# A decoder block on one core: the masked key planes of cross-attention made by GpSimd from one ScalarE copy

## The chip, the cores and the metric

One core of a Trainium2 chip runs the whole kernel. The metric is the device time of one execution in microseconds (us); lower is better. Three executions of the kernel before took 1203.84, 1200.0 and 1203.6 us, median 1203.6.

## The reference, cut to what matters

128 sequences of 64 tokens, width 128, all fp32. Three sublayers, each on a layer norm of x and added back to x:

```python
x = x + agent_attention(layernorm(x))          # 16 heads of 64, 8 pooled agents
x = x + cross_attention(layernorm(x), ctx)     # 16 heads of 8, causal
x = x + moe(layernorm(x))                      # gate, top 2 of 16 experts, 2 shared experts

# cross attention
Q, K, V = split(query @ Wq.T), split(key @ Wk.T), split(value @ Wv.T)   # (B, 16, 64, 8)
scores = Q @ K^T / sqrt(8) + causal
out = softmax(scores) @ V, heads joined, @ Wo.T
```

The change is in how K reaches the scores.

## The kernel before

**Groups.** The work is cut into 8 groups of 16 sequences (1024 tokens). The function `both(e, g)` of each engine runs one step of a two-stage pipeline: group g passes through both attentions while group e = g - 1 passes through the experts. So there are 9 steps: one with g = 0 alone, seven with both, one with e = 7 alone. Each engine (PE, DVE, ACT, POOL, and SP for loads) has its own fixed order written out by hand, and the engines meet through semaphores. An engine that waits holds everything behind it on its own queue.

**PSUM rings.** Results of PE lie in eight banks, shared out in rings. The ring "att" has four banks; `KT_0` and `KT_1` (the transposed keys, 128 x 512 each, all 16 heads by 8 rows) are two of its tenants. PE may fill a bank again when the semaphore in the table `read` says that the tenant before has been read: for `KT_n` that is `Kx_ready`.

**Keys.** The score matmuls (L602 to L605) contract over 32 rows at a time, in which four heads of 8 rows lie. So that a head meets only its own 8 rows, K is stored four times, in planes `Kx[:, j, :]` of the tile `KQ` (planes 0 to 3), each with the rows of the other heads set to zero and those of its own scaled by 8^-0.5. ScalarE makes them in `K_moved(g, n)` (L869 to L877): for each half n (512 tokens), four `activation(Copy)` from PSUM with a scale of one value per partition, `plane[:, j]`. The queries go to `Qx`, plane 4 of `KQ`, in `Q_moved` (L900), late in the step.

**Order on ACT** around the keys: ctxT, V and xnT1 moves; `K_moved(g, 0)`; `M_moved` 0 to 3 (moments of agent attention); the two xnT3 moves with their fp32r roundings (L940, L941); `M_moved` 4; the exponential of the gate (L946); `M_moved` 5 to 7; `silu(e, 0)`; `K_moved(g, 1)`; `silu(e, 1)`; the move of combS.

**Order on PE**: `keys_of(g, 0)` (L660), `moments` 0 to 3 (L668), xnT3, moment 4, gate logits (L708), moments 5 to 7, `unit(e, 0)` (L488 to L490), agent scores (L538, L549), `keys_of(g, 1)`, `up(e, 1)`, `down_to(e, 0)` (L507), then the transposes of combS (L726), which wait for `comb_ready`, and with combsT back from ACT the expert units 1, 2, 3 and on.

**Order on DVE**: add_x, the norms (L1036 to L1046), pooled (L1229), xn3, `gate_shift` (L1058), `gate` (L1066 to L1117), then `soften(g, 0)` (L1144) and the hidden units. `gate(e)` picks the top two experts in a serial chain of some thirty small instructions; after L1083 it runs `hidden(e, 0)` (L1128), which waits for `silu(e, 0)`. Its last instruction, L1117, raises `comb_ready`. Most of its instructions are `tensor_tensor` with both inputs in SBUF:

```python
link_e(V.tensor_tensor(orig[:], gex[:], g2[:].unsqueeze(2).to_broadcast(te), ALU.mult))   # L1075
link_e(V.tensor_tensor(sc[:], orig[:], gb[:].unsqueeze(1).to_broadcast(te), ALU.add))     # L1076
```

Their `link` is a semaphore wait of DVE on its own instruction.

**Order on POOL**: the power for the norm of g (L393), the power for the norm of e (L396), the low parts of xnT3 (L400, two halves), `xr = xin + bo` (L409), store 0 of e (L388), a power (L415), store 1, then the 32 normalisations of the cross-attention probabilities (L423).

Of the kernel before, what the change touches and what calls it, by code (L numbers as in the profile page):

```python
# [6 lines left out]
def decoder_block(nc, x, ctx_in, Wqkv, Wo_a, bo, Wq, Wk, Wv, Wo_x, gate_w, gate_b,  # L7
# [14 lines left out]
    ALU, ACT, AX = mybir.AluOpType, mybir.ActivationFunctionType, mybir.AxisListType.X  # L22

    B, S, D = x.shape
    P = 128
# [14 lines left out]
    CH = 512  # L40
# [39 lines left out]
    with ExitStack() as ctx:  # L80
# [3 lines left out]
        def sem(name):  # L84
            return ctx.enter_context(nc.semaphore(name))
# [127 lines left out]
        var3_ready, rstd3_ready, xn3_ready, xnT3_ready = (  # L213
            sem("var3_ready"), sem("rstd3_ready"), sem("xn3_ready"), sem("xnT3_ready"))
        w_split, hi_ready, lo_ready = sem("w_split"), sem("hi_ready"), sem("lo_ready")
        ctxT_ready, Kx_ready, V_ready = sem("ctxT_ready"), sem("Kx_ready"), sem("V_ready")
        pooled_ready, M_ready = sem("pooled_ready"), sem("M_ready")
        d1_ready, d2_ready, e1_ready, e2_ready = sem("d1_ready"), sem("d2_ready"), sem("e1_ready"), sem("e2_ready")
        p2_ready, p1T_ready, p2T_ready = sem("p2_ready"), sem("p1T_ready"), sem("p2T_ready")
# [14 lines left out]
                "combT_1": (combT_ready, 3, 2)}  # L234
        for n in range(2):
            read |= {f"xnT1_{n}": (xnT_ready, 4, n), f"xnT2_{n}": (xnT_ready, 4, 2 + n),
                     f"xnT3_{n}": (hi_ready, 2, n), f"ctxT_{n}": (ctxT_ready, 2, n), f"KT_{n}": (Kx_ready, 2, n),
                     f"QT_{n}": (Qx_ready, 2, n), f"Y_{n}": (out_ready, 2, n), f"s2_{n}": (d2_ready, 2, n),
                     f"p1T_{n}": (p1T_ready, 2, n), f"p2T_{n}": (p2T_ready, 2, n), f"Ya_{n}": (attn_added, 2, n)}
        for n in range(4):  # L240
# [19 lines left out]
        def ps(name):  # L260

            return bank[place[name][0]][place[name][1]]
# [15 lines left out]
        def wait_full(eng, g, name):  # L278

            ring, k, use, per, _ = place[name]  # L280
            eng.wait_ge(full[ring, k], g * per + use + 1)
# [54 lines left out]
        @block.gpsimd  # L336
        def _(pool):
            steps = [0]

            def step(ins):  # L340
                steps[0] += 1
                ins.then_inc(const_step, 1)
                pool.wait_ge(const_step, steps[0])

            step(nc.gpsimd.memset(b2x[:], 0.0))
            nc.gpsimd.memset(mhalf[:], -0.5).then_inc(consts, 1)
            nc.gpsimd.memset(ident[:], 0.0)
            nc.gpsimd.memset(onehot3[:], 0.0)
            nc.gpsimd.memset(pick[:], 0.0)
            nc.gpsimd.memset(maskb[:], 0.0)  # L350
            nc.gpsimd.memset(beats[:], 0.0)
            step(nc.gpsimd.memset(planes[:], X_SCALE))

            step(nc.gpsimd.affine_select(out=ident[:], in_=ident[:], compare_op=ALU.not_equal, fill=1.0, base=0,
                                         pattern=[[-1, P]], channel_multiplier=1))
            nc.gpsimd.tensor_copy(identb[:], ident[:]).then_inc(consts, 1)
            nc.gpsimd.memset(woM[:], 0.0)
            nc.gpsimd.memset(Vb[:], 0.0)
            nc.gpsimd.memset(xnT[:, TOK:TOK + S], 0.0)
            nc.gpsimd.memset(combs[:], 0.0)  # L360
            nc.gpsimd.memset(combT[:], 0.0)
            step(nc.gpsimd.memset(comb[:], 0.0))
            nc.gpsimd.memset(comb[:, :, E:E + 1], 1.0)
            nc.gpsimd.iota(down[:], pattern=[[-1, E]], base=E, channel_multiplier=0,
                           allow_small_or_imprecise_dtypes=True)

            for k in range(3):
                step(nc.gpsimd.affine_select(out=onehot3[:], in_=onehot3[:], compare_op=ALU.not_equal, fill=1.0,
                                             base=-E * k, pattern=[[-1, E]], channel_multiplier=1))

            step(nc.gpsimd.affine_select(out=planes[:], in_=planes[:], compare_op=ALU.is_ge, fill=0.0, base=0,
                                         pattern=[[-XC, 4], [-4 * XC, 4]], channel_multiplier=1))
            step(nc.gpsimd.affine_select(out=planes[:], in_=planes[:], compare_op=ALU.is_ge, fill=0.0, base=XC - 1,
                                         pattern=[[XC, 4], [4 * XC, 4]], channel_multiplier=-1))
            for q in range(XQ):
                rr = slice(32 * q, 32 * q + 32)
                for a in range(2):
                    step(nc.gpsimd.affine_select(out=maskb[rr, a], in_=maskb[rr, a], compare_op=ALU.is_ge, fill=MASKED,
                                                 base=32 * a, pattern=[[0, HALF], [-1, S]], channel_multiplier=1))
                    step(nc.gpsimd.affine_select(out=pick[rr, a], in_=pick[rr, a], compare_op=ALU.not_equal, fill=1.0,  # L380
                                                 base=32 * a, pattern=[[-1, S]], channel_multiplier=1))
            nc.gpsimd.tensor_copy(spread[:].rearrange("r p a i -> r (p a) i"),
                                  onehot3[:].unsqueeze(2).to_broadcast([P, E, EI])).then_inc(consts, 1)

            def store(e, c):
                pool.wait_ge(out_ready, CHUNKS * e + c + 1)
                dst = o_v[e] if isinstance(e, int) else o_v[bass.ds(e, 1)].rearrange("a p t d -> (a p) t d")
                pool.dma_start(dst[:, QT * c:QT * c + QT, :], xo[:, QT * c:QT * c + QT, :]).then_inc(stored, 16)  # L388

            def both(e, g):  # L390
                if g is not None:
                    pool.wait_ge(var_ready, 2 * g + 1)
                    nc.gpsimd.tensor_tensor(rstda[:], va[:], mhalf[:], ALU.pow).then_inc(rstd_ready, 1)  # L393
                if e is not None:
                    pool.wait_ge(var3_ready, e + 1)
                    nc.gpsimd.tensor_tensor(rstdb[:], vb[:], mhalf[:], ALU.pow).then_inc(rstd3_ready, 1)  # L396
                    for n in range(2):
                        half = slice(512 * n, 512 * n + 512)
                        pool.wait_ge(hi_ready, 2 * e + n + 1)
                        nc.gpsimd.tensor_tensor(xnT3l[:, half], xnT3[:, half], xnT3h[:, half].bitcast(fp32),  # L400
                                                ALU.subtract).then_inc(lo_ready, 1)
                if g is not None:

                    pool.wait_ge(xn_ready, 2 * g + 1)
                    if e is not None:
                        pool.wait_ge(xattn_added, UX * g)
                    else:
                        pool.wait_ge(loaded_m, 16 * 10)
                    nc.gpsimd.tensor_tensor(xr[:], xin[:], bo_b[:].unsqueeze(1).to_broadcast([P, T, D]),  # L409
                                            ALU.add).then_inc(xr_ready, 1)  # L410
                if e is not None:
                    store(e, 0)
                if g is not None:
                    pool.wait_ge(var_ready, 2 * g + 2)
                    nc.gpsimd.tensor_tensor(rstda[:], va[:], mhalf[:], ALU.pow).then_inc(rstd_ready, 1)  # L415
                if e is not None:
                    store(e, 1)
                if g is not None:
                    for k in range(XQ * UX):
                        u, q = k // XQ, k % XQ  # L420
                        pool.wait_ge(rx_ready, 2 * UX * g + k // 2 + 1)
                        p = pr[k % PR]
                        nc.gpsimd.tensor_tensor(p, p, rx[:, u % 2, q].unsqueeze(2).to_broadcast([P, HALF, S]),  # L423
                                                ALU.mult).then_inc(pn_ready, 1)

            run(pool, both)
            pool.wait_ge(stored, 16 * CHUNKS * GROUPS)


        @block.tensor  # L430
        def _(pe):
# [240 lines left out]
            def both(e, g):  # L672
# [116 lines left out]
                    pe.wait_ge(loaded_m, 16 * 10)  # L789
                    pe.wait_ge(w_split, 4)  # L790
                if g is not None:
                    pe.wait_ge(Kx_ready, 2 * g + 2)
                    pe.wait_ge(V_ready, 4 * g + 4)
                    scores(g, 0)
                if e is not None:
# [22 lines left out]
        def _(act):  # L818
# [50 lines left out]
            def K_moved(g, n):  # L869

                if isinstance(g, int) and g == 0:
                    act.wait_ge(w_split, 4)
                wait_full(act, g, f"KT_{n}")
                for j in range(4):
                    last = nc.scalar.activation(Kx[:, j, 512 * n:512 * n + 512], ps(f"KT_{n}")[:], ACT.Copy,
                                                scale=plane[:, j:j + 1])
                last.then_inc(Kx_ready, 1)  # L877

            def V_moved(g, n):

# [18 lines left out]

            def Q_moved(g, n):  # L900

                moved(g, f"QT_{n}", Qx[:, 512 * n:512 * n + 512], Qx_ready)

            def exp_x(g, k):
# [411 lines left out]
```

## Time and profile before

| | |
|---|---|
| median of 3 executions | 1203.6 us (1200.0 to 1203.84) |
| the profiled execution, its own time | 1206.25 us |
| its span in the profile | 1204.3 us |
| busy: PE | 980.4 us, 81% |
| busy: DVE | 778.2 us, 65% |
| busy: ACT | 578.7 us, 48% |
| busy: POOL | 237.2 us, 20% |
| mean granted TensorE clock | 0.918 of full speed |

The span is the time between the first and the last instruction; the profiled execution's own time is 1.95 us longer. Seven steps with both stages take about 140 us each. A row of a timeline gives the start, the time from the start of the first to the end of the last instruction of the row, the engine, the line of the kernel, the operation, output and input tile, the count, and in brackets how long the engine stood idle before and what released it.

### The profile page before, as it was taken

What the parts mean: (1) busy time and instruction counts of PE and PEld (TensorE: products, weight loads), DVE (VectorE), ACT (ScalarE), POOL (GpSimd) and SP (SyncE); (2) the same over time, 40 slices, a digit from 0 to 9 for tenths busy, and PEclk for the clock granted to TensorE, in tenths of its full rate; (3) what the DMA queues carried; (4) which work ended last, traced back from release to release, by engine and by line L of the source; (5) the groups of instructions that cost most, each with busy time, mean ns of one, the idle gap of its engine ahead of it and who ended that gap; (6) DMA issues with size and microseconds to landing.
All of it is one profiled execution on the core that took longest, in us unless ns stands there. A gap on an engine that the chain in (4) does not pass through costs nothing.

```text
span 1204.3 us, 24165 instructions
## 1 busy us (share of the span) xinstructions
PE 980.4 (81%) x9023; PEld 777.9 (65%) x9069; DVE 778.2 (65%) x1825; ACT 578.7 (48%) x1148; POOL 237.2 (20%) x236
## 2 busy tenths in 40 slices
PE   6656889968898688977899688977899778996677
PEld 5543678747785477845787376855778457874466
DVE  3356766675657767676666857677676766668454
ACT  4434645365444564355553664445643564536222
POOL 6001410043000520014100440005200241004200
PEclk9887889988899898989899898998989898998789
DMA  5300010000100010000100001000100000000000
GB/s 141 76 1 1 2 36 1 10 10 3 36 9 10 2 37 1 10 10 3 36 1 10 10 3 36 10 10 3 37 1 10 10 4 1 1 10 9 1 1 18
DMA packets 28925, 18.64 MB, mean 15 GB/s; under 512 B 7649, under 2 KB 27394, under 8 KB 28802
## 3 DMA queue, kind: packets, MB, share of 16 engines
q1 hardware_dynamic: 26914, 12.48, 3.9%
q0 software_dynamic: 1280, 4.20, 1.1%
q8 instruction: 84, 1.38, 0.5%
q14 instruction: 39, 0.32, 0.1%
q10 hardware_dynamic: 608, 0.27, 0.1%
HBM read 12.62 MB, written 4.19 MB: 14 GB/s over the span
## 4 chain that ended last, share of the span: by engine, by line
PE 48%; DVE 17%; issue 17%; POOL 9%; ACT 6%; SPq 1%; DMA 0%; DVEq 0%; POOLq 0%; ACTq 0%
PE banks L507 8%; PE banks L488 6%; PE banks L668 5%; POOL PXUT L423 5%; PE banks L490 4%; PE banks L489 4%; PE banks L750 2%; POOL KQ L423 2%; DVE stats_a L1036 2%; DVE mx L1183 2%; PE banks L578 2%; DVE lx L1195 2%; PE banks L497 1%; PE banks L708 1%; PE banks L538 1%
## 5 line engine op out<-in xcount | busy, mean ns | idle before, releaser
L855 ACT ACTIVATE sil<-banks,b 128x512 f32<-128x512 f32 x144 | 99.6, 692 | 209.6 <-PE banks L490 207.5
L1131 DVE SCALAR_TENSOR_TENSOR sil<-banks,b,sil 128x512 f32<-128x512 f32 x128 | 95.9, 749 | 102.1 <-ACT sil L855 90.0
L507 PEld LDWEIGHTS banks<-w,hT 128*128 128x128 f32 x1152 | 156.6, 198 | 7.8 <-issue 2.7
L507 PE MATMUL banks<-w,hT 128*128 128x128 f32 x1152 | 156.9, 280 | 3.1 <-DVE hT L1135 0.5
L848 ACT COPY M<-banks 128x512 f32<-128x512 f32 x208 | 125.0, 613 | 32.3 <-PE banks L668 15.5
L388 POOL DMA_DIRECT2D out_x<-xn x16 | 12.9, 809 | 565.6 <-DVE xn L1141 565.6
L423 POOL TENSOR_TENSOR PXUT<-PXUT,rx 128x512 f32<-128x512 f32 x96 | 97.0, 1040 | 126.9 <-DVE rx L1197 126.9
L1135 DVE TENSOR_TENSOR hT<-sil,banks 128x512 f32<-128x512 f32 x128 | 87.9, 687 | 19.1 <-DVE sil L1131 3.3
L618 PE MATMUL banks<-ident,PXUT 128*128 128x128 f32 x384 | 66.2, 311 | 36.7 <-ACT M L848 32.0
L488 PE MATMUL banks<-xnT3l,w1h 128*128 128x512 f32 x144 | 78.0, 542 | 12.7 <-ACT combsT L848 10.3
L618 PEld LDWEIGHTS banks<-ident,PXUT 128*128 128x128 f32 x384 | 46.1, 155 | 58.5 <-POOL PXUT L423 35.4
L595 PE MATMUL banks<-maskb,pick 32*64 32x512 bf16 x512 | 42.2, 504 | 48.7 <-ACT PXUT L911 27.6
L668 PE MATMUL banks<-pooled,A 128*128 128x128 f32 x512 | 66.5, 290 | 16.1 <-DVE pooled L1229 16.1
L668 PEld LDWEIGHTS banks<-pooled,A 128*128 128x128 f32 x512 | 63.2, 204 | 22.7 <-DVE pooled L1229 22.7
L1183 DVE TENSOR_REDUCE mx<-banks 128x8 f32<-128x512 f32 x96 | 65.2, 679 | 0.0
L488 PE MATMUL banks<-xnT3l,w3h 128*128 128x512 f32 x144 | 61.1, 425 | 4.6 <-DVE sil L1131 4.6
L911 ACT ACTIVATE PXUT<-banks,mx 128x64 f32<-128x64 f32 x192 | 42.0, 330 | 46.0 <-DVE mx L1181 46.0
L848 ACT COPY PXUT<-banks 128x512 f32<-128x512 f32 x64 | 36.0, 588 | 54.8 <-PE banks L578 32.5
L1195 DVE TENSOR_REDUCE lx<-PXUT 128x8 f32<-128x512 f32 x96 | 59.6, 662 | 0.0
L1201 DVE TENSOR_TENSOR xe<-xr,banks 128x256 f32<-128x256 f32 x32 | 13.4, 420 | 71.2 <-PE banks L642 53.8
L490 PE MATMUL banks<-xnT3h,w1h 128*128 128x512 f32 x144 | 59.1, 410 | 0.0
L490 PE MATMUL banks<-xnT3h,w3h 128*128 128x512 f32 x144 | 59.0, 410 | 0.0
(197 smaller groups left out, 2102.4 us busy)
## 6 DMA issues: line engine op xcount, KB each, us to landing
xin<-in_x SPq DMA_DIRECT2D x8, 512.0 KB, 3.9
cin<-in_ctx SPq DMA_DIRECT2D x8, 512.0 KB, 5.0
out_x<-xn POOLq DMA_DIRECT2D x16, 256.0 KB, 2.8
KQ<-in_L_attn_Wqkv SPq DMA_DIRECT2D x3, 512.0 KB, 5.1
KQ<-in_L_ffn_We SPq DMA_DIRECT2D x2, 512.0 KB, 4.6
KQ<-in_L_attn_Wo SPq DMA_DIRECT2D x1, 512.0 KB, 7.7
w<-in_L_ffn_We SPq DMA_DIRECT2D x1, 512.0 KB
woM<-xwT SPq DMA_DIRECT2D x16, 8.0 KB, 1.8
```

What stands on the lines that cost most here:

```text
L423: nc.gpsimd.tensor_tensor(p, p, rx[:, u % 2, q].unsqueeze(2).to_broadcast([P, HALF, S]), ALU.mult).then_inc(pn_ready, 1)
L488: mm(ps(name)[:], wh[:, 2 * p:2 * p + 2, :], xl, start=True, stop=False)
L490: mm(ps(name)[:], wh[:, 2 * p:2 * p + 2, :], xh, start=False, stop=True).then_inc(fulled(name), 1)
L507: mm(ps(name)[:, P * t:P * t + P], hT[:, k % 2, P * t:P * t + P], w2[:, pair[k], :], start=(n == 0 and t == 0), stop=False, skip_group_che ...
L618: last = turn_over(ps(name)[:, P * j:P * j + P], src[:, P * j:P * j + P], ident[:])
L668: last = mm(ps(f"M_{n}")[:, P * k:P * k + P], A[:, 4 * (n % 4) + k, :], pooled[:], start=True, stop=True)
L848: cp(dst, ps(name)[:] if src is None else src).then_inc(ready, 1)
L855: nc.scalar.activation(sil[:, k % 2, :], ps(f"H1_{k}")[:], ACT.Silu, bias=b1[:, pair[k]:pair[k] + 1]).then_inc(sil_ready, 1)
L1131: V.scalar_tensor_tensor(sil[:, k % 2, :], ps(f"H3_{k}")[:], b3[:, p:p + 1], sil[:, k % 2, :], ALU.add, ALU.mult).then_inc(hid_ready, 1)
L1135: V.tensor_tensor(hT[:, k % 2, :], sil[:, k % 2, :], ps(f"C_{k}")[:], ALU.mult).then_inc(hT_ready, 1)
L1183: link(V.tensor_reduce(mx[:, q], sv, AX, ALU.max), g)
L1195: last = V.tensor_reduce(lx[:, u % 2, q], pr[k % PR], AX, ALU.add)
```

## The change

ScalarE copies `KT_n` once, unmasked, into the half n of `Qx`, where this group's queries come only later. GpSimd multiplies that copy with the plane's column, spread over 512 tokens, four times per half, into `Kx`. The move of the queries (`Q_moved(g, 0)`) now waits for all eight products, since it overwrites their input. The PSUM bank of `KT_n` comes free with the one copy (`K_ready`). In POOL's order the products stand behind `xr` and ahead of store 0.

```diff
-                     f"xnT3_{n}": (hi_ready, 2, n), f"ctxT_{n}": (ctxT_ready, 2, n), f"KT_{n}": (Kx_ready, 2, n),
+                     f"xnT3_{n}": (hi_ready, 2, n), f"ctxT_{n}": (ctxT_ready, 2, n), f"KT_{n}": (K_ready, 2, n),
...
+            def spread_K(g, n):
+
+                pool.wait_ge(K_ready, 2 * g + n + 1)
+                half = slice(512 * n, 512 * n + 512)
+                for j in range(4):
+                    nc.gpsimd.tensor_tensor(Kx[:, j, half], Qx[:, half],
+                                            plane[:, j:j + 1].to_broadcast([P, CH]), ALU.mult).then_inc(Kx_ready, 1)
+
             def both(e, g):
+                if isinstance(g, int) and g == 0:
+                    pool.wait_ge(plane_ready, 1)
...
                     nc.gpsimd.tensor_tensor(xr[:], xin[:], bo_b[:].unsqueeze(1).to_broadcast([P, T, D]),
                                             ALU.add).then_inc(xr_ready, 1)
+                    spread_K(g, 0)
+                    spread_K(g, 1)
                 if e is not None:
                     store(e, 0)
...
-                    pe.wait_ge(Kx_ready, 2 * g + 2)
+                    pe.wait_ge(Kx_ready, 8 * g + 8)
                     pe.wait_ge(V_ready, 4 * g + 4)
                     scores(g, 0)
...
-                wait_full(act, g, f"KT_{n}")
-                for j in range(4):
-                    last = nc.scalar.activation(Kx[:, j, 512 * n:512 * n + 512], ps(f"KT_{n}")[:], ACT.Copy,
-                                                scale=plane[:, j:j + 1])
-                last.then_inc(Kx_ready, 1)
+                moved(g, f"KT_{n}", Qx[:, 512 * n:512 * n + 512], K_ready)
...
             def Q_moved(g, n):
 
+                if n == 0:
+                    act.wait_ge(Kx_ready, 8 * g + 8)
                 moved(g, f"QT_{n}", Qx[:, 512 * n:512 * n + 512], Qx_ready)
```

## Rows read from the trace of the kernel before

**Rows 1.** The page: busy times, and the chain's shares by engine.
```profile
PE 980.4 (81%) x9023; PEld 777.9 (65%) x9069; DVE 778.2 (65%) x1825; ACT 578.7 (48%) x1148; POOL 237.2 (20%) x236
...
PE 48%; DVE 17%; issue 17%; POOL 9%; ACT 6%; SPq 1%; DMA 0%; DVEq 0%; POOLq 0%; ACTq 0%
```

**Rows 2.** The chain in order of time, 555 to 625 us: start, us, what.
```profile
572.29 3.85 PE banks L668 x32
...
592.79 0.30 DVE combs L1117
```

**Rows 3.** Source L1117, the last instruction of the gate: who waited.
```profile
  PE banks L726: 23.7, 8
```

**Rows 4.** Timeline of PE, 555 to 612 us, around its wait for the gate.
```profile
593.22 1.01 PE L726 MATMUL banks<-identb,combs 128*128 128x128 bf16 x8 [2.68 <-DVE combs L1117]
595.54 0.90 PE L488 MATMUL banks<-xnT3l,w1h 128*128 128x512 f32 x1 [1.30 <-ACT combsT L848]
```

**Rows 5.** Windows of 2 us: busy times, then TensorE's granted clock.
```profile
593.00:595.00 2.00, 1.01 (x8) 0.78 (x8) 1.93 (x6) 0.73 (x1) 0.00 (x0) 0.50 0.00 0
...
601.00:603.00 2.00, 2.00 (x16) 1.65 (x15) 0.99 (x2) 0.69 (x1) 0.00 (x0) 1.00 0.00 0
```

**Rows 6.** Source L875, the key copies: ns min/median/max.
```profile
L875 ACT ACTIVATE KQ<-banks,plane x64: 679/688/698, 43.5 to 1009.8; 128x512 f32<-128x512 f32 x64
```

**Rows 7.** Timeline of ACT, 572 to 592 us.
```profile
571.49 2.42 ACT L875 ACTIVATE KQ<-banks,plane 128x512 f32<-128x512 f32 x4
...
576.17 0.59 ACT L848 COPY M<-banks 128x512 f32<-128x512 f32 x1 [0.31 <-PE banks L668]
...
588.30 2.42 ACT L875 ACTIVATE KQ<-banks,plane 128x512 f32<-128x512 f32 x4 [2.67 <-PE banks L660]
```

**Rows 8.** POOL's groups by line and shape: busy, mean ns, idle before.
```profile
L423 POOL TENSOR_TENSOR PXUT<-PXUT,rx 128x512 f32<-128x512 f32 x96 | 97.0, 1040 | 126.9 <-DVE rx L1197 126.9
...
L400 POOL TENSOR_TENSOR xnT3l<-xnT,xnT3h 128x512 fp32r<-128x512 f32 x16 | 19.9, 1265 | 39.6 <-ACT xnT3h L941 39.6
```

**Rows 9.** Timeline of POOL, 555 to 620 us.
```profile
557.02 4.04 POOL L423 TENSOR_TENSOR PXUT<-PXUT,rx 128x512 f32<-128x512 f32 x4 [4.27 <-DVE rx L1197]
...
580.26 2.36 POOL L409 TENSOR_TENSOR xr<-xin,bo_b 128x1024 f32<-128x1024 f32 x1
```

**Rows 10.** Timeline of POOL, 580 to 650 us: store 0.
```profile
632.81 0.81 POOL L388 DMA_DIRECT2D out_x<-xn  x1 [50.19 <-DVE xn L1141]
```

**Rows 11.** Timeline of DVE, 555 to 612 us: the gate and what follows.
```profile
581.82 0.94 DVE L1075 TENSOR_TENSOR gate<-gate,g 128x128 f32<-128x128 f32 x1
582.80 0.29 DVE L1076 TENSOR_TENSOR gate<-gate,gb 128x128 f32<-128x128 f32 x1
...
585.66 0.75 DVE L1128 SCALAR_TENSOR_TENSOR hT<-banks,b,sil 128x512 f32<-128x512 f32 x1 [1.53 <-ACT sil L855]
...
588.17 0.29 DVE L1103 TENSOR_TENSOR oh<-gate,g 128x128 f32<-128x128 f32 x1
588.49 0.29 DVE L1104 TENSOR_TENSOR oh<-oh,down 128x128 f32<-128x128 f32 x1
...
595.89 0.74 DVE L1131 SCALAR_TENSOR_TENSOR sil<-banks,b,sil 128x512 f32<-128x512 f32 x1
```

**Rows 12.** Sources L1075 and L1184 (one PSUM input): ns min/median/max.
```profile
L1075 DVE TENSOR_TENSOR gate<-gate,g x8: 291/945/960, 158.0 to 1140.5; 128x128 f32<-128x128 f32 x8
...
L1184 DVE TENSOR_TENSOR PXUT<-banks,mx x72: 691/691/692, 98.6 to 1106.2; 128x512 f32<-128x512 f32 x72
```

**Rows 13.** Timeline of DVE, 1140 to 1142 us, the last step: no POOL instruction runs.
```profile
1140.53 0.29 DVE L1075 TENSOR_TENSOR gate<-gate,g 128x128 f32<-128x128 f32 x1
```

**Rows 14.** Timeline of the first step, 38 to 68 us.
```profile
58.67 2.42 ACT L875 ACTIVATE KQ<-banks,plane 128x512 f32<-128x512 f32 x4 [3.34 <-PE banks L660]
...
64.06 0.69 DVE L1164 TENSOR_TENSOR PXUT<-PXUT,r 128x512 f32<-128x512 f32 x1
```

**Rows 15.** Timeline of ACT, 648 to 664 us: the move of the queries.
```profile
656.32 0.59 ACT L848 COPY KQ<-banks 128x512 f32<-128x512 f32 x1 [2.00 <-PE banks L784]
```

More of the change, by code:

```diff
@@ L215, in decoder_block @@
         w_split, hi_ready, lo_ready = sem("w_split"), sem("hi_ready"), sem("lo_ready")
-        ctxT_ready, Kx_ready, V_ready = sem("ctxT_ready"), sem("Kx_ready"), sem("V_ready")
+        ctxT_ready, K_ready, Kx_ready, V_ready = sem("ctxT_ready"), sem("K_ready"), sem("Kx_ready"), sem("V_ready")
         pooled_ready, M_ready = sem("pooled_ready"), sem("M_ready")
```

## The prediction

> **What bounds the kernel now.** I read the page first. No engine is full: PE 81%, DVE 65%, ACT 48%, POOL 20% [rows 1]. So busy time freed on ACT is worth something only where ACT is what is waited for. The chain that ended last gives ACT 6% and POOL 9% of the span, PE and DVE most of it [rows 1]. Next I read the chain in order of time through one middle step (seven of the nine are alike, about 140 us each). Ahead of the expert units it runs PE's moments, a short piece of ACT, the first silu, and then the serial chain of the gate on DVE down to L1117 [rows 2]. The reader should see that the key copies are no piece of it. The source view of L1117 says who is at its far end: PE's transposes of combS, eight times, 23.7 us in all [rows 3]. In PE's timeline this is 2.68 us of standing still, then 1.30 us more for combsT [rows 4]. PE has nothing else in its order to do there. Whatever lengthens the gate on DVE lengthens the step by as much. TensorE's granted clock is at half (1.2 GHz) from 593 us, in this gap and on into the first expert unit behind it, and back at full (2.4 GHz) after 601 us [rows 5].
>
> **Removed from ACT.** 64 copies of 688 ns [rows 6] in 16 groups of four; a group takes 2.42 us [rows 7]. One copy takes 0.59 us, as the move of M_3 beside it [rows 7]. That frees 1.83 us per half, 16 x 1.83 = 29 us of ACT. Where would it be felt?
> - Half 0 (571.49 us) stands ahead of the moves of the moments. By M_3 ACT has caught up: it stood idle 0.31 us for PE before that move, and that move is the next piece of the chain [rows 7]. Freeing 1.83 us ahead of an engine that waits anyway gives nothing. I take 0; the cover is PE's 3.85 us of moments [rows 2].
> - Half 1 (588.30 to 590.72 us) stands ahead of the second silu [rows 7]. DVE takes that silu up only at 595.89 us, behind the gate [rows 11]. I take 0; the cover is the gate, five us of it.
> The bound from the other side, if one of the two were felt in full in each of eight groups, is 8 x 1.83 = 15 us gained.
>
> **Added to POOL.** 8 products per group, 64 in all. The nearest row is L423: the same shape, also with a factor that stays the same along the row, 1040 ns, and four in a row take 4.04 us [rows 8, 9]. The other end is L400, two dense inputs, 1265 ns [rows 8]. I take 1.04 us, since the plane's factor is constant along the row. 64 x 1.04 = 67 us of busy time; POOL has room for it.
>
> **Where they run, and what waits.** In a middle step POOL does `xr` from 580.26 to 582.62 us and then nothing until store 0 at 632.81 us [rows 9, 10]. Products 1 to 4 follow `xr` at once, their input being long there; 5 to 8 follow the second copy, 588.30 + 0.59, so from about 588.95 us. Even at 1265 ns all is over near 600 us. Behind them wait store 0, over 30 us later, and the queries' move at 656.32 us [rows 10, 15]. Both new waits cost 0; the cover is over 50 us of expert units for the queries.
>
> **What the products do to DVE.** Here is the price. L1075, the first gate instruction that reads two SBUF tensors, takes 945 ns in the median and 291 ns at least [rows 12]. The short one is the last, in the step in which POOL does nothing [rows 13]. In the middle step it starts at 581.82 us and ends at 582.76 us; `xr` on POOL ends at 582.62 us [rows 9, 11]. So DVE was held until POOL's instruction had ended, and finished 0.14 us later. L1076, with POOL idle, takes its 0.29 us again [rows 11]. The Trainium skill says so as a rule, in SBUF — State Buffer, section Who interferes with whom: a VectorE instruction with two SBUF inputs and a GpSimd instruction that reads SBUF exclude each other, and the one that issues second blocks fully. By that rule, with which the trace agrees in the one place where it can be seen, every product holds or is held; the same section also names tensor_scalar in a two-port mode, which would make L1097 one more victim and change the sum by less than 1 us per step. The subtractions of L1184 take one input from PSUM, run beside L423 all through the softmax, and lie within 691 to 692 ns [rows 12]. So only the ones with both inputs in SBUF count; from L1075 to L1117 that is most of the chain.
>
> Product by product. Undisturbed, one such instruction follows the other in 0.32 us (588.17 to 588.49 us [rows 11]). With a product between them it is 1.04 us of waiting and the 0.14 us of finishing, during which the next product waits its turn: 1.18 us. That is 0.86 us for each product that meets a waiting two-input instruction, 8 x 0.86 = 6.9 us. From this comes off:
> - DVE stood idle 1.53 us for the first silu, ahead of L1128 [rows 11]. The first four products can eat that: -1.5 us.
> - Some products run partly beside a one-input instruction (the reductions, about 0.3 us each, every third instruction). I count three: -0.9 us.
> Left are 4.5 us per step. It goes on at full length: L1117 ends 4.5 us later, PE stands 7.2 us in place of 2.68, and everything after it (PE units, exponentials, softmax) is behind. In the clock I expect no more lost than now: it already falls in this gap and returns with the work [rows 5].
>
> Who is served first between two products is not to be seen in the trace. If products that follow one another keep DVE out until the fourth is done, DVE stands 4.04 us twice; less the 1.5 us of idle time it is 6.5 us per step. If DVE were served first nearly always, and each product only filled gaps, a lost start here and there would be left, 2 us per step. I take 4.5, since L1075 has waited before the next product asks.
>
> **First step.** No gate runs. Products 1 to 4 fall where DVE is idle. Products 5 to 8 run from 58.67 + 0.59 = 59.3 to 63.4 us, and the first two-input instruction, L1164, starts at 64.06 us [rows 14]. Cost 0; the chain there is on PE and DVE, not on ACT. Last step: no keys, no product, cost 0. So seven steps count.
>
> **The sum.** 0 for ACT, 7 x 4.5 = +31.5 us. The profiled execution took 1206.25 us, so 1237.8 us by its own time; it stands 2.65 us above the median of the three runs. On the median of 1203.6 us that is 1235 us, 2.6% slower.
>
> **The rivals.**
> - Locked out twice per step: 7 x 6.5 = 45.5, so 1249 us. For it: products in a row would start about 1.0 us apart and take 1.04 [rows 8, 9], so there is hardly a gap between them. Against: the held instruction asked first. Products of 1265 ns add 8 x 0.22 x 7 = 12 us to the forecast and end in the same place.
> - Gaps only: 7 x 2 = 14, so 1218 us. For it: small instructions in a row without waits between them (L1089 and on) may keep POOL out rather than be kept out.
> - No change, 1204 us: the hold of L1075 would be something about `xr` alone, or the products would fall beside L1083, the silu wait and L1128 only. The idle 1.53 us covers one and a half products, not eight, which speaks against it.
> - Faster, 1189 us: DVE isn't held, and ACT's 1.83 us is felt once per group. It decides only if M_3 or the second silu is what PE or DVE waits for, and both show a wait the other way [rows 7, 11]. With part of it the time is 1195 us.
>
> **Chances.** Forecast mechanism, 4 to 5.5 us per step: 45%. Locked out: 24%. Gaps only: 17%. No change: 8%. Faster: 6%. A measurement of this kernel can tell about 0.3%, 3.6 us, from no change. Faster 0.06, same 0.08, slower 0.86. The range leaves out the last two cases and the far end of the lock-out with dense-priced products: 1212 to 1256 us (gaps only less some, locked out and 7 us more).
>
> **What would show each step.** Right: key moves on ACT 16 copies of 0.59 us; 64 products of 1.04 us on POOL, four from about 582.7 in each step and four from about 589; many two-input instructions between L1076 and L1108 at 0.9 to 1.1 us in place of 0.29; one-input ones at their old length; PE's idle time before L726 near 7 us; middle steps near 144.5 us; first and last steps as they were. Wrong: gate instructions at 0.29 us while products run, PE's wait before L726 unchanged, or PE waiting somewhere else, such as for the scores' keys.

## The result, and the profile after

The changed kernel takes 1241.88 us (median of 4, 1235.32 to 1247.53) against 1203.72 us before: a ratio of 1.032 with an interval of 1.026 to 1.038. It is slower, as forecast, and 6.9 us beyond the forecast of 1235 us. The profiled execution took 1244.5 us with a span of 1242.9 us.

Here PE is TensorE, DVE VectorE, ACT ScalarE and POOL GpSimd. Lines of the changed kernel stand 10 or 12 further down: the gate's L1075 is L1085 there, L1076 is L1086, PE's L726 is L738, the moments' L668 is L680. The page of the changed kernel: span, busy times and the group of the products (busy time, mean ns, idle time before):

```profile
span 1242.9 us, 24189 instructions
...
PE 1001.5 (81%) x9023; PEld 798.3 (64%) x9069; DVE 817.3 (66%) x1825; ACT 553.1 (45%) x1100; POOL 303.1 (24%) x300
...
L395 POOL TENSOR_TENSOR KQ<-KQ,plane 128x512 f32<-128x512 f32 x64 | 66.2, 1063 | 49.8 <-ACT KQ L860 49.8
```

ACT lost 26 us of work and POOL gained 66 us, near the 29 and 67 worked out. DVE has the same 1825 instructions and 39 us more of "busy" time [rows 1]. This is the first thing to see, and it has to be read with care, for PE too has the same 9023 instructions and 21 us more. PE's instructions take longer at a lower granted clock (0.891 of full speed in the mean, 0.918 before). DVE's are held by something, and the time for which an instruction is held counts as busy.

The timeline of DVE in a middle step of the changed kernel shows where:

```profile
594.88 0.94 DVE L1085 TENSOR_TENSOR gate<-gate,g 128x128 f32<-128x128 f32 x1
595.86 1.01 DVE L1086 TENSOR_TENSOR gate<-gate,gb 128x128 f32<-128x128 f32 x1
596.91 0.95 DVE L1089 TENSOR_TENSOR ps<-gate 128x64 f32<-128x64 f32 x1
597.77 1.08 DVE L1090 TENSOR_TENSOR ps<-gate 128x64 f32<-128x64 f32 x1
598.78 1.07 DVE L1091 TENSOR_TENSOR ps<-gate 128x32 f32<-128x32 f32 x1
599.76 0.21 DVE L1092 TENSOR_TENSOR ps<-gate 128x32 f32<-128x32 f32 x1
600.00 0.35 DVE L1093 TENSOR_REDUCE gs<-ps 128x32 f32<-128x192 f32 x1
600.60 0.75 DVE L1138 SCALAR_TENSOR_TENSOR hT<-banks,b,sil 128x512 f32<-128x512 f32 x1 [0.24 <-DVE gs L1093]
...
604.07 0.78 DVE L1116 TENSOR_TENSOR oh<-oh,g 128x128 f32<-128x128 f32 x1
604.88 1.01 DVE L1118 SCALAR_TENSOR_TENSOR gate<-oh,gate 128x128 f32<-128x128 f32 x1
605.93 0.29 DVE L1112 TENSOR_REDUCE g<-gate 128x8 f32<-128x128 f32 x1
606.25 0.69 DVE L1113 TENSOR_TENSOR oh<-gate,g 128x128 f32<-128x128 f32 x1
606.98 1.01 DVE L1114 TENSOR_TENSOR oh<-oh,down 128x128 f32<-128x128 f32 x1
```

And POOL in the same stretch:

```profile
593.32 2.36 POOL L419 TENSOR_TENSOR xr<-xin,bo_b 128x1024 f32<-128x1024 f32 x1
595.63 4.14 POOL L395 TENSOR_TENSOR KQ<-KQ,plane 128x512 f32<-128x512 f32 x4
603.66 4.18 POOL L395 TENSOR_TENSOR KQ<-KQ,plane 128x512 f32<-128x512 f32 x4 [3.89 <-ACT KQ L860]
```

Read the two together. While the four products run, four instructions of DVE that read two SBUF tensors take 0.95 to 1.08 us, one per product. The first of them took 0.29 us before [rows 11]; L1092, which comes through after the last product, shows with 0.21 us what the small ones need. A reduction reads one tensor: L1112, at 605.93 us and so beside a product of the second four, keeps its 0.29 us. Of the 1.53 us that DVE stood idle ahead of L1128 [rows 11], 0.24 us are left ahead of L1138. From the start of L1086 to that of L1138 the time is 4.74 us where it was 2.86 from L1076 to L1128, so +1.88. From L1099 (601.26 us) to the last instruction L1127 (610.05 us) it is 8.79 us where it was 6.46, so +2.33. Together the gate is 4.2 us longer. The instructions are held for 5.5 us per gate, since another 1.3 us took the place of idle time; seven times 5.5 is DVE's 39 us of busy time. PE's wait for it, as the source view of L1127 gives it, is 43.5 us where it was 23.7 [rows 3]:

```profile
  PE banks L738: 43.5, 8
```

That is 20 us more and not 7 x 4.2 = 29. In the first gate PE waits the full 7.14 us; in the six others it waits 5.25 us, because it comes to the wait later. Its last 24 matmuls of the moments, ahead of the first expert unit, take 1.63 us longer there than before. The rows of PE are the wait in the first gate, then the moments and the wait in the middle step:

```profile
171.50 1.01 PE L738 MATMUL banks<-identb,combs 128*128 128x128 bf16 x8 [7.14 <-DVE combs L1127]
...
593.15 4.55 PE L680 MATMUL banks<-pooled,A 128*128 128x128 f32 x24
...
610.49 1.01 PE L738 MATMUL banks<-identb,combs 128*128 128x128 bf16 x8 [5.25 <-DVE combs L1127]
```

The same moments in the kernel before:

```profile
580.08 2.92 PE L668 MATMUL banks<-pooled,A 128*128 128x128 f32 x24
```

This raises a rival for the first half of the gate. The slower moments make the first silu late, and DVE waits for that silu ahead of L1138. Is the +1.88 us the hold's, or the silu's? In the middle step both are there: the silu ends at 600.32 us, DVE's own chain at 600.35 us. The first gate separates them. There the moments took 2.92 us as before, and from L1085 to L1138 DVE still took 5.71 us, as against 5.72 us in the middle step and 3.84 us in the kernel before. So the hold alone makes the delay, and the late silu hides behind it.

The step as a whole can be cut at marks that both kernels have: the start of the moments, of PE's combS transposes, and of the first product of probabilities by POOL.

```
stretch                                     before    after
moments to combS transposes, PE             20.93     25.13    +4.20
combS transposes to first probabilities     80.41     80.79    +0.38
first probabilities to the next moments     38.60     40.87    +2.27
one middle step                            139.94    146.79    +6.85
```

The last 2.3 us lie in a stretch in which no product of the keys runs. The windows view shows what is different there (busy times of PE, PEld, DVE, ACT and POOL, then the granted clock). The changed kernel, from 700 us, the start of a step with its first transposes at 717.9 us:

```profile
700.00:716.00 16.00, 11.37 (x168) 8.83 (x160) 10.54 (x21) 9.20 (x22) 7.99 (x9) 0.89 0.01 2
716.00:724.00 8.00, 6.07 (x34) 5.33 (x36) 3.03 (x17) 3.45 (x6) 4.59 (x4) 0.57 0.02 4
724.00:740.00 16.00, 14.40 (x199) 12.58 (x195) 8.66 (x34) 10.01 (x22) 3.96 (x3) 1.00 0.01 3
740.00:744.00 4.00, 4.00 (x23) 4.00 (x23) 3.32 (x7) 1.48 (x3) 4.00 (x4) 0.59 0.04 12
```

and the kernel before in the same part of a step, first transposes at 559.7 us:

```profile
559.00:567.00 8.00, 6.81 (x116) 5.97 (x118) 4.22 (x21) 5.10 (x11) 3.73 (x4) 1.00 0.02 6
567.00:580.00 13.00, 11.04 (x116) 9.55 (x112) 7.24 (x30) 9.70 (x20) 3.83 (x3) 1.00 0.01 2
580.00:584.00 4.00, 4.00 (x32) 3.79 (x32) 3.15 (x11) 2.42 (x5) 2.62 (x2) 1.00 0.02 7
```

Two stretches that ran at 2.4 GHz now run near 1.2 GHz: the first transposes of the step, and the last moments. Only the first of them is paid beside the gate. From the first transposes to the output matmuls behind them PE now needs 5.44 us (571.11 to 576.55 us) where it needed 3.43 us (559.68 to 563.11 us), 2.0 of the 2.3 us:

```profile
571.11 1.94 PE L478 MATMUL banks<-ident,cin 128*128 128x128 f32 x8 [3.00 <-issue]
...
576.55 1.24 PE L654 MATMUL banks<-woM,KQ 128*64 128x128 f32 x16
```

and before:

```profile
559.68 1.06 PE L466 MATMUL banks<-ident,cin 128*128 128x128 f32 x8 [2.65 <-issue]
...
563.11 1.09 PE L642 MATMUL banks<-woM,KQ 128*64 128x128 f32 x16
```

The last moments' 1.63 us lie beside the gate, behind the hold, and cost this kernel nothing. The kernel before has this pair in one of its own steps, the first with a full step behind it, which took 144.05 us and not 140:

```profile
276.00:283.00 7.00, 6.26 (x38) 5.53 (x40) 2.80 (x16) 3.52 (x6) 3.32 (x3) 0.54 0.01 4
299.00:303.00 4.00, 4.00 (x24) 4.00 (x23) 3.17 (x11) 1.48 (x3) 2.24 (x1) 0.57 0.03 9
```

So there are two questions for the runs: is it the products' reading of SBUF that holds DVE, and where do the 2.6 us per step beyond the gate come from?

### The profile page after: what moved, and what is told of

It is laid out like the page before. It is cut to its first block, busy times and chain, and to the rows that moved or that the text cites. A ratio compares the mean times of both kernels' runs of the same rounds, so it can differ in the third digit from the quotient of the medians.

```text
span 1242.9 us, 24189 instructions
## 1 busy us (share of the span) xinstructions
PE 1001.5 (81%) x9023; PEld 798.3 (64%) x9069; DVE 817.3 (66%) x1825; ACT 553.1 (45%) x1100; POOL 303.1 (24%) x300
## 4 chain that ended last, share of the span: by engine, by line
PE 50%; DVE 19%; issue 15%; POOL 8%; ACT 6%; SPq 1%; DMA 0%; DVEq 0%; POOLq 0%; ACTq 0%
PE banks L519 8%; PE banks L500 5%; PE banks L502 4%; PE banks L501 4%; POOL PXUT L435 4%; PE banks L630 3%; PE banks L680 3%; PE banks L654 3%; PE banks L762 2%; DVE mx L1193 2%; POOL KQ L435 2%; PE banks L478 2%; PE banks L641 1%; PE banks L590 1%; PE banks L509 1%
## 5 line engine op out<-in xcount | busy, mean ns | idle before, releaser
L630 PE MATMUL banks<-ident,PXUT 128*128 128x128 f32 x384 | 74.5, 343 | 33.9 <-ACT M L860 30.3
L630 PEld LDWEIGHTS banks<-ident,PXUT 128*128 128x128 f32 x384 | 54.1, 175 | 55.6 <-POOL PXUT L435 34.1
L680 PE MATMUL banks<-pooled,A 128*128 128x128 f32 x512 | 73.4, 309 | 19.1 <-DVE pooled L1239 19.1
L680 PEld LDWEIGHTS banks<-pooled,A 128*128 128x128 f32 x512 | 70.1, 222 | 25.7 <-DVE pooled L1239 25.7
L395 POOL TENSOR_TENSOR KQ<-KQ,plane 128x512 f32<-128x512 f32 x64 | 66.2, 1063 | 49.8 <-ACT KQ L860 49.8
L860 ACT COPY KQ<-banks 128x512 f32<-128x512 f32 x64 | 37.8, 591 | 80.6 <-PE banks L641 32.7
```

Source lines behind the costliest of these rows:

```text
L395: nc.gpsimd.tensor_tensor(Kx[:, j, half], Qx[:, half], plane[:, j:j + 1].to_broadcast([P, CH]), ALU.mult).then_inc(Kx_ready, 1)
L630: last = turn_over(ps(name)[:, P * j:P * j + P], src[:, P * j:P * j + P], ident[:])
L680: last = mm(ps(f"M_{n}")[:, P * k:P * k + P], A[:, 4 * (n % 4) + k, :], pooled[:], start=True, stop=True)
L860: cp(dst, ps(name)[:] if src is None else src).then_inc(ready, 1)
```

## The experiments

**1. The products behind the gate.** The eight products are left as they are and only wait until the gate is done.

```diff
+                    if e is not None:
+                        pool.wait_ge(comb_ready, e + 1)
                     spread_K(g, 0)
                     spread_K(g, 1)
```

> The changed kernel, but GpSimd waits for the end of the gate (comb_ready) before the eight products, in the steps that have a gate; same 64 products, same single copies on ScalarE. Theory (the products hold DVE's two-input instructions of the gate, ScalarE's relief is worth nothing): L1075 keeps its 0.94 us, because of xr, all others of the gate are back at 0.29 us, PE's idle time before the combS transposes is 2.7 us again, time 1200 to 1208 us. Rival (the time went to the new waits or to the products' load on GpSimd as such): 1235 to 1247 us as with the change. Rival (ScalarE's relief is worth something and was hidden by the hold): under 1196 us.

1200.67 us (10 runs, 1197.67 to 1209.43); ratio to before 0.9985, interval 0.995 to 1.002. The timeline of POOL has the eight products in a row, the timeline of DVE the gate with only L1087 (the old L1075) held, by `xr`:

```profile
584.75 8.02 POOL L395 TENSOR_TENSOR KQ<-KQ,plane 128x512 f32<-128x512 f32 x8 [10.56 <-DVE combs L1129]
```
```profile
573.39 0.95 DVE L1087 TENSOR_TENSOR gate<-gate,g 128x128 f32<-128x128 f32 x1
574.38 0.29 DVE L1088 TENSOR_TENSOR gate<-gate,gb 128x128 f32<-128x128 f32 x1
```

The same 64 products cost 38 us beside the gate and nothing that can be measured behind it. The new waits of PE and of the queries' move cost nothing either.

**2. ScalarE's relief alone.** `spread_K` isn't called, PE waits for the copies; the masked planes are not made, so the scores are those of other data.

```diff
-                    spread_K(g, 0)
-                    spread_K(g, 1)
...
-                    pe.wait_ge(Kx_ready, 8 * g + 8)
+                    pe.wait_ge(K_ready, 2 * g + 2)
...
-                if n == 0:
-                    act.wait_ge(Kx_ready, 8 * g + 8)
```

> The changed kernel without the products: ScalarE copies the keys once and nothing makes the masked planes, so the scores are those of whatever lies in the planes; PE waits for the copy instead. This is ScalarE's relief alone. Theory: 1200 to 1207 us, no gain. Rival (ScalarE's 1.83 us per half are felt): 1189 to 1196 us.

1203.99 us (10 runs), ratio 0.9997, interval 0.997 to 1.002. The 29 us freed on ScalarE are worth nothing.

**3. The relief taken away, the products kept.**

```diff
+                wait_full(act, g, f"KT_{n}")
+                for j in range(4):
+                    nc.scalar.activation(Kx[:, j, 512 * n:512 * n + 512], ps(f"KT_{n}")[:], ACT.Copy,
+                                         scale=plane[:, j:j + 1]).then_inc(Ka_ready, 1)
                 moved(g, f"KT_{n}", Qx[:, 512 * n:512 * n + 512], K_ready)
...
                 pool.wait_ge(K_ready, 2 * g + n + 1)
+                pool.wait_ge(Ka_ready, 8 * g + 4 * n + 4)
```

> The changed kernel with ScalarE's four masked copies kept as well, ahead of the plain copy; GpSimd's products then overwrite the planes with the same values. ScalarE has 0.6 us more per half than before the change, 2.4 us more than with it. Theory (only the products matter): 1235 to 1250 us as with the change, the second four products start about 2.4 us later, so a few hundred ns per step either way. Rival (ScalarE's relief gave back part of a larger loss): 1250 to 1262 us.

1237.02 us (4 runs), ratio 1.027, interval 1.021 to 1.033. The loss stands or falls with the products, not with ScalarE's part.

**4. GpSimd writes, but doesn't read.** Each product becomes a memset of the same plane, which leaves the cross-attention scores out; a product of one column carries the wait.

```diff
-                for j in range(4):
-                    nc.gpsimd.tensor_tensor(Kx[:, j, half], Qx[:, half],
-                                            plane[:, j:j + 1].to_broadcast([P, CH]), ALU.mult).then_inc(Kx_ready, 1)
+                nc.gpsimd.tensor_tensor(tiny[:, n:n + 1], Qx[:, 512 * n:512 * n + 1], plane[:, 0:1], ALU.mult)
+                for j in range(4):
+                    nc.gpsimd.memset(Kx[:, j, half], 0.0).then_inc(Kx_ready, 1)
```

> The changed kernel with each product replaced by a GpSimd memset of the same plane and half (and one product of a single column ahead of each four, that reads the copy); the masked planes are zeros, so the cross-attention scores are left out. GpSimd writes SBUF but does not read it, 4 x about 0.53 us per half. Theory by the Trainium skill (SBUF - State Buffer, section Who interferes with whom: a two-input VectorE instruction contends with a GpSimd instruction that reads SBUF, not with one that only writes): gate instructions at 0.29 us while the memsets run, 1200 to 1208 us. Rival (any GpSimd instruction holds DVE): gate instructions of 0.5 to 0.6 us beside the memsets, some 1 to 2 us per step, 1211 to 1220 us.

1203.53 us (10 runs), ratio 0.999, interval 0.996 to 1.002. Timelines of POOL and of DVE in this run, in which L1087 is the old L1076, and L1090 and L1091 the old L1079 and L1080:

```profile
577.64 0.24 POOL L395 TENSOR_TENSOR tiny<-KQ,plane 128x1 f32<-128x1 f32 x1
577.83 1.92 POOL L397 MEMSET KQ<- 128x512 f32 x4
```
```profile
577.87 0.29 DVE L1087 TENSOR_TENSOR gate<-gate,gb 128x128 f32<-128x128 f32 x1
578.20 0.23 DVE L1090 TENSOR_TENSOR ps<-gate 128x64 f32<-128x64 f32 x1
578.34 0.22 DVE L1091 TENSOR_TENSOR ps<-gate 128x64 f32<-128x64 f32 x1
```

Two-input instructions of DVE take the same 0.22 to 0.29 us beside memsets as with GpSimd idle. So GpSimd's being busy, or its writing to SBUF, doesn't hold them. A memset differs from a product in more than the reading (it is another instruction, and four take 1.92 us, not 4.14), so that the reading is the cause is the simplest account and not shown by this run alone. The Trainium skill, in SBUF — State Buffer, section Who interferes with whom, states it so: a VectorE instruction with two SBUF inputs contends with a GpSimd instruction that reads SBUF, not with one that only writes it. This trace agrees.

**5. Half of the products behind the gate.**

```diff
                     spread_K(g, 0)
+                    if e is not None:
+                        pool.wait_ge(comb_ready, e + 1)
                     spread_K(g, 1)
```

> The changed kernel with the second four products put behind the gate (GpSimd waits for comb_ready before them), the first four left where the change has them. In the changed kernel's trace the first four cost 1.9 us per step at the start of the first silu's consumer, the second four 2.3 us. Theory (each product that meets a two-input instruction holds it): half the loss in the gate, 1.9 us per step, 13 us in all, so 1215 to 1225 us with what the clock adds. Rival (the first four vanish in the 1.5 us of idle time): 1200 to 1208 us. Rival (the first four carry nearly all): 1230 us or more.

1223.32 us (4 runs), ratio 1.016, interval 1.012 to 1.020: half the loss. The first four don't vanish in the idle time. Seven gates of 1.9 us make 13 us; 19 were measured, so here too there is more than the gate.

**6 and 7. `xr` out of the gate as well.** In the one run the wait for `comb_ready` stands ahead of `xr` and all products; in the other it is added to the kernel before, ahead of `xr` alone.

```diff
+                    if e is not None:
+                        pool.wait_ge(comb_ready, e + 1)
                     pool.wait_ge(xn_ready, 2 * g + 1)
```

> The changed kernel with xr = xin + bo and all eight products behind the gate. xr holds L1075's successor in the gate for 0.65 us in seven steps before and after the change; xr is needed only by the addition of the attention's result some 45 us later, and by the next load of x. Theory: L1075's successor takes 0.29 us, but 1.5 us of idle time for the first silu stand behind it, so the 0.65 us only lengthen that idle time: no gain over the products behind the gate, 1197 to 1206 us. Rival (the 0.65 us reach the end): 7 x 0.65 = 4.6 us less than the kernel before, 1195 to 1200 us.

> The kernel before with xr alone moved behind the gate: L1075 takes 0.29 us, and by the theory the 0.65 us are swallowed by the idle time ahead of L1128, 1200 to 1207 us. Rival: 1195 to 1200 us.

1203.95 us (12 runs, ratio 0.999, interval 0.996 to 1.002) and 1204.3 us (12 runs, ratio 0.999, interval 0.997 to 1.002). A hold of 0.65 us that ends ahead of an idle time of 1.5 us is free. None of the versions beats the kernel before by more than the intervals allow.

**8 and 9. DVE late by itself.** In the kernel before, more reductions whose value nothing reads are put into the gate behind L1128, 18 in one run and 13 in the other. GpSimd and ScalarE are not touched.

```diff
                 hidden(e, 0)
+                for _ in range(18):
+                    link_e(V.tensor_reduce(g3[:], gex[:], AX, ALU.add))
...
-        LINKS_A, LINKS_E = 40, 28
+        LINKS_A, LINKS_E = 40, 46
```

> The kernel before, nothing moved, with 18 more reductions of 128 x 128 in the gate ahead of L1128 (each 0.32 us from start to start, writing a value that nothing reads): 5.8 us less 1.5 us of idle time, a delay of 4.3 us per gate, also in the last step, and no GpSimd instruction involved. This tests what the changed kernel's step pays beyond the gate: its step is 7.0 us longer, its gate only 4.2 us. Theory (the delay itself moves TensorE's work against its granted clock, and the low stretches at the start of the step come with the delay): steps of 146 to 147 us, 1240 to 1252 us. Rival (the further 2.8 us come from GpSimd or ScalarE work): steps of 144.2 us, 1232 to 1238 us.

> The kernel before with 13 more reductions of 0.32 us in the gate, behind L1128 (where the idle time for the first silu is already over), so 4.2 us per gate in all eight gates, no GpSimd instruction involved: the same delay that the changed kernel's products put on its seven. In the run with 18 reductions they turned out to stand behind L1128 as well, and 5.76 us of direct delay made steps 7.5 us longer. Theory (a delay of the gate moves TensorE's later work under more low stretches of its granted clock): steps 5.5 to 7.5 us longer than 140, 1246 to 1262 us. Rival (the surplus of the changed kernel's step over its gate's 4.2 us is GpSimd's or ScalarE's): steps of 144.2 us, 8 x 4.2 = 34 us, 1238 us.

With 18: 1274.33 us (4 runs), ratio 1.059, interval 1.055 to 1.064. I had placed them wrongly in my expectation: they stand behind the idle time, so each gate is late by the full 5.76 us and not by 4.3. Eight gates make 46 us; 70 were measured, above both ranges of the expectation. With 13: 1243.11 us (4 runs), ratio 1.033, interval 1.030 to 1.037. Eight gates of 4.2 us make 34 us; 39 were measured. PE's waits at two neighbouring steps of this run:

```profile
318.23 1.01 PE L726 MATMUL banks<-identb,combs 128*128 128x128 bf16 x8 [6.86 <-DVE combs L1119]
...
465.42 1.01 PE L726 MATMUL banks<-identb,combs 128*128 128x128 bf16 x8 [6.84 <-DVE combs L1119]
```

The wait is the same in each step, 6.85 us, 4.2 more than before. The steps are not: from combS to combS they take 143.9, 147.2, 147.1, 143.3, 143.3 and 143.4 us. Against 139.9 us, four are 3.4 to 4.0 us longer, about the delay, and two are 7.2 or 7.3 us longer, with GpSimd's products out of it. The theory's 5.5 to 7.5 us held for two of the six; the other four fit the rival, and the time lies between the two forecasts. In just the two long steps the last moments took 4.55 us and not 2.92. With no hold to hide behind, their 1.63 us are paid: the first silu is late, and the gate takes 16.8 us from L1075 to its end, not 15.1. What is shown: a late gate alone can bring steps as long as those of the changed kernel, at a lower mean clock (0.900 against 0.918 of the profiles). What isn't shown: why some steps get it and others don't, and whether the products have a part in giving it to all gates but the first in the changed kernel.

**10. Finer products.** Each is cut into two of 256 columns.

```diff
-                for j in range(4):
-                    nc.gpsimd.tensor_tensor(Kx[:, j, half], Qx[:, half],
-                                            plane[:, j:j + 1].to_broadcast([P, CH]), ALU.mult).then_inc(Kx_ready, 1)
+                for j in range(4):
+                    for a in range(2):
+                        part = slice(512 * n + 256 * a, 512 * n + 256 * a + 256)
+                        last = nc.gpsimd.tensor_tensor(Kx[:, j, part], Qx[:, part],
+                                                       plane[:, j:j + 1].to_broadcast([P, 256]), ALU.mult)
+                    last.then_inc(Kx_ready, 1)
```

> The changed kernel with each product cut into two of 256 columns: 16 per step instead of 8, the same columns in all, at the same place. Theory (a two-input instruction of DVE waits until the GpSimd instruction in progress ends, then runs, then the next one of GpSimd): DVE gets one instruction through per 0.55 us instead of per 1.05 us, so a held instruction costs about 0.25 us more than its 0.32; 16 x 0.25 less the 1.3 us of idle time and a few reductions is some 2 us per step instead of 4.2, so 1217 to 1230 us. Rival (each hold costs the same 0.73 us whatever its size): over 1260 us. Rival (only the GpSimd time as a whole counts): 1240 to 1247 us.

In the gate of one middle step the timeline of DVE agrees with the theory (L1088 is the old L1076, L1129 the last of the gate):

```profile
595.69 0.94 DVE L1087 TENSOR_TENSOR gate<-gate,g 128x128 f32<-128x128 f32 x1
596.67 0.59 DVE L1088 TENSOR_TENSOR gate<-gate,gb 128x128 f32<-128x128 f32 x1
...
609.10 0.29 DVE L1129 TENSOR_TENSOR combs<-gate,combs 128x128 bf16<-128x128 f32 x1
```

Held instructions take 0.59 us, not 1.01, and L1087 to L1129 is 13.41 us: 2.4 us more than before the change (10.97) instead of 4.2. But only two of the seven gates are like this one. In the other five the last moments ran at half clock, and the shorter hold no longer hides the late silu:

```profile
456.02 0.75 DVE L1140 SCALAR_TENSOR_TENSOR hT<-banks,b,sil 128x512 f32<-128x512 f32 x1 [1.26 <-ACT sil L869]
```

Those gates take 14.5 us, 3.5 more than before the change. The time doesn't agree with the theory either: 1243.15 us (4 runs), ratio 1.032, interval 1.028 to 1.035, the same as with whole products. By the time alone the rival that only the GpSimd time as a whole counts would fit too; the 0.59 us speak against it. The steps take 144.1 to 147.1 us and the mean clock is 0.877, the lowest of all profiles here. The expected 1217 to 1230 us left the clock out. Where it went can be read from single steps, cut at the starts of PE's first transposes, of its moments and of its combS transposes. The steps end at 733.17 us (before), 757.27 us (changed), 899.12 and 465.42 us (experiment 9) and 465.48 us (experiment 10):

```
from, to                        before   changed   9, short   9, long   10, long
combS to first transposes       106.66    107.44     106.08    107.30     109.30
first transposes to moments      12.35     14.22      12.12     13.16      13.15
moments to combS                 20.94     25.12      25.11     26.73      24.46
step                            139.95    146.78     143.31    147.19     146.91
```

Three steps of about 147 us are three different sums. The finer products give back 0.7 us between moments and combS and 1.1 us in the transposes, and lose 1.9 us in the expert units, softmax and what else lies ahead of the transposes.

## Why the prediction was right

**The bound and the place.** The gate of DVE was the path: seven waits of PE for it grew, and that of the last step did not (4.90 and 4.92 us). As a meter the wait was read wrongly. The forecast had it near 7 us in each step, and it was so in one gate only (7.14 us); in six it was 5.25 us, since PE itself came 1.63 us later at the lower clock. And that the step grows by as much as the gate did not hold: 4.2 us of gate went with 6.8 us of step, 146.8 us and not the 144.5 that were to be the sign.

**ScalarE at 0.** Right, by experiments 2 and 3. In the changed kernel ACT still stands idle 0.31 us ahead of M_3's move, and the second silu is ready (604.38 us) before the gate is even over.

**The products.** Forecast 1.04 us, measured 1.06 us in the mean, with a median of 1.08; the new waits at 0, right by experiment 1.

**The hold.** That a two-input instruction waits for the product in progress and gets through before the next was the step with the least evidence, one instruction in the trace before. It is what the trace after shows, product for product; neither lock-out nor "gaps only" is to be seen. Nothing in the trace before decided between it and the lock-out, and it had 45%: that it came out was a good guess and not a proof. The price per hold was a little too high: I took 1.18 us from one to the next; they are 1.05 us (595.86 to 596.91 us), so 0.73 us more than the 0.32, not 0.86. The first four products hold one instruction each in full and add 3.2 us; the second four add 0.49, 0.72, 0.40 and 0.72 us, which is the 2.33 us. From this come off the 1.3 of the 1.5 us of idle time that were eaten. Together 4.2 us per step against a forecast of 4.5.

**The term that was off.** "In the clock I expect no more lost than now." The steps are 6.8 us longer, not 4.2. Of the 2.6 us beyond the gate, 2.0 lie in the first transposes, where the granted clock has newly fallen to half; 0.4 us lie between the combS transposes and the first probabilities. At 7 x 4.2 the time would have been 1233 us. That the lower clock follows from the late gate is shown for two steps of experiment 9 and argued for the changed kernel; what decides which steps get it stays open. The spans of the two profiled executions differ by 38.6 us: five steps by 6.8 to 7.0 us each, one by only 1.4 us, since that step of the kernel before had its slow stretches already, and the beginning and end by 2.7 us together. Against 4.5 us forecast for each of seven, the five long steps are 12 us above it in all, the short one 3 us below, and the beginning and end 2 us below: 7 us short in the sum. So part of the closeness is luck. Had all seven cost 6.8 us, the forecast would have been 16 us short.

## What to carry to other kernels

Before moving elementwise work to GpSimd because it is idle, look at what DVE does in those microseconds: instructions that read two SBUF tensors stopped here for each GpSimd product that ran beside them, 0.7 us each, and a chain of small ones on the critical path is a bad neighbour for them. The same products placed some ten microseconds later, beside DVE instructions that read PSUM, cost nothing. And judge relief of an engine by who waits for it, not by its busy time: 29 us of ScalarE were worth 0. Last, when two engines meet at one point, a delay of one can hide a delay of the other: here the hold covered 1.63 us of slower moments, and the finer products uncovered them.

## What the runs showed of the hardware that was not expected

- One instruction with a single SBUF input was held too. L1107, a tensor_scalar of 32 columns, has 181 ns in the median and 855 ns once, in the first gate, where a product was running (from 162.78 us). The prediction had named this line, L1097 there, as one more possible victim at under 1 us per step. In the middle step it runs at 602.24 us, between the two fours, so that it says little that it keeps its 0.18 us there:

```profile
L1107 DVE TENSOR_SCALAR kb<-rank x8: 181/181/855, 163.0 to 1182.3; 128x32 f32<-128x32 f32 x8
```

- Time lost in one place of this kernel is paid in uneven amounts. 4.2 us of delay per step gave steps 3.4 to 4.0 or 7.2 to 7.3 us longer (experiment 9); products that hold DVE for less gave the same time (experiment 10); and the kernel before itself has two lengths of its early steps, 144.05 us in one profile, 139.97 us in the profile of experiment 7, which differs only in where `xr` runs. The runs of the kernel before spread over 1197.6 to 1209.6 us with it. In the long steps of the kernel before and of experiments 9 and 10 the last moments ran near half clock and took 4.6 us, and the first transposes took 1.0 to 2.0 us longer; in the short ones neither did.
